# VectorE's block transposes in place of TensorE's for attention outputs and token rows

## The reference, cut to what matters

```python
xn = (x - mean) / sqrt(var + 1e-5)
# linear attention, 16 heads of 8, 64 features a head
q, k, v = heads(xn @ Wq + bq), heads(xn @ Wk + bk), heads(xn @ Wv + bv)
qp = relu(einsum('bhsd,hdf->bhsf', q, rw)) + 1e-6
kp = relu(einsum('bhsd,hdf->bhsf', k, rw)) + 1e-6
kv = einsum('bhsf,bhsd->bhfd', kp, v)
out = einsum('bhsf,bhfd->bhsd', qp, kv) / (einsum('bhsf,bhf->bhs', qp, kp.sum(2)) + 1e-6)
attn = out.reshape(b, s, 128) @ Wo + bo
# eight experts (128 -> 512 -> 128), each row goes to its best one
probs = softmax(xn @ wr + br); top_p, top_i = top_k(probs, 2)
gate = top_p[:, 0] / (top_p[:, 0] + top_p[:, 1])
ffn = gate * (gelu(xn @ w1[e] + b1[e]) @ w2[e] + b2[e])   # e = top_i[:, 0]
result = x + attn + ffn
```

## Time and profile before

| | us |
|---|---|
| median of 3 runs | 228.54 (228.49 to 228.83) |
| the profiled execution | 229.5 |
| its span, first to last instruction | 227.5 |

### The profile page before, as it was taken

One profiled execution on the slowest core, in us unless ns is written; L12 is line 12 of the kernel. 1 busy time (PEld: TensorE's weight loads), 2 busy tenths in 40 slices (PEclk: granted clock), 3 DMA queues, 4 the chain that ended last, 5 costly groups with the idle time before them and its releaser, 6 DMA issues. The chain is left out here.

```text
span 227.5 us, 6689 instructions
## 1 busy us (share of the span) xinstructions
PE 198.3 (87%) x2267; PEld 159.3 (70%) x2267; DVE 130.9 (58%) x420; ACT 124.0 (55%) x293; POOL 141.7 (62%) x165
## 2 busy tenths in 40 slices
PE   0399899589999999999999999999999999999930
PEld 0256466456666666666666666999999999999930
DVE  5737735959876667665665575345544455444420
ACT  3167797345654455544555565856666666666600
POOL 1847863022267777777777711018888888888885
PEclk9999999969999999999999999999999999999995
DMA  4945999950011111111112654168999999999331
GB/s 128 286 127 150 200 132 288 303 133 1 4 38 60 55 48 43 58 61 58 54 58 69 201 128 146 48 214 166 179 205 204 211 210 200 211 205 208 58 35 9
DMA packets 32191, 29.53 MB, mean 130 GB/s; under 512 B 5504, under 2 KB 24480, under 8 KB 32160
## 3 DMA queue, kind: packets, MB, share of 16 engines
q1 hardware_dynamic: 24752, 24.14, 40.6%
q0 software_dynamic: 6640, 4.24, 13.7%
q10 hardware_dynamic: 768, 0.74, 1.1%
HBM read 20.17 MB, written 11.49 MB: 139 GB/s over the span
## 5 line engine op out<-in xcount | busy, mean ns | idle before, releaser
L397 POOL DMA_INDIRECT out<-k_all,slots_all x39 | 61.0, 1563 | 25.4 <-DVE k_all L938 18.4
L715 ACT ACTIVATE q_all<-feat,w_slot 128x128 f32<-128x128 f32 x156 | 44.6, 369 | 28.4 <-PE feat L563 17.1
L372 POOL DMA_INDIRECT sorted_x<-rows_all,place_i x32 | 31.7, 990 | 15.6 <-PE kv_bank L471 8.4
L563 PE MATMUL feat<-v_all,w_slot 128*128 128x128 f32 x312 | 41.3, 275 | 0.0
L563 PEld LDWEIGHTS feat<-v_all,w_slot 128*128 128x128 f32 x312 | 38.0, 192 | 0.1
L672 ACT ACTIVATE k_feat<-feat 128x1024 f32<-128x1024 f32 x16 | 16.4, 1025 | 28.0 <-PE feat L449 28.0
L861 DVE TENSOR_SCALAR q_feat<-feat 128x1024 f32<-128x1024 f32 x16 | 19.6, 1225 | 16.2 <-PE feat L460 16.1
L679 ACT ACTIVATE q_feat<-feat 128x1024 f32<-128x1024 f32 x16 | 16.4, 1026 | 19.0 <-PE feat L460 19.0
L328 POOL TENSOR_SCALAR rows_all<-x_all,meanvar,rstd 128x128 f32<-128x128 f32 x23 | 18.7, 822 | 11.7 <-DVE rstd L747 11.7
L854 DVE TENSOR_SCALAR k_feat<-feat 128x1024 f32<-128x1024 f32 x16 | 19.6, 1224 | 10.6 <-PE feat L449 10.6
L460 PE MATMUL feat<-q_all,rw_bd 32*128 32x256 f32 x256 | 19.0, 411 | 7.4 <-DVE k_feat L854 7.4
(11 more groups left out here) (118 smaller groups left out, 313.0 us busy)
## 6 DMA issues: line engine op xcount, KB each, us to landing
w_slot<-w1x SPq DMA_DIRECT2D x39, 258.0 KB
sorted_x<-ones_f SPq DMA_DIRECT2D x1, 2535.0 KB, 17.6
x_all<-in_x SPq DMA_DIRECT2D x8, 256.0 KB, 3.8
w1x<-in_w SPq DMA_DIRECT2D x1, 2048.0 KB, 24.2
out<-res SPq DMA_DIRECT2D x16, 128.0 KB, 1.7
slots_all<-sorted_x SPq DMA_DIRECT2D x23, 65.0 KB
out<-k_all,slots_all POOLq DMA_INDIRECT x39
slots_all<-sorted_x SPq DMA_DIRECT2D x1, 520.0 KB, 5.8
```

Source lines behind the costliest of these rows:

```text
L372: pool.indirect_dma_start(sorted_x, bass.IndirectOffsetOnAxis(ap=place_i[:, t:t + 1], axis=0), rows_all[:, t, :], None).then_inc(x_moved, 16)
L397: pool.indirect_dma_start(out_rows, bass.IndirectOffsetOnAxis(ap=slot_rows[j % SLOT_RING][:, D + 1:XW].bitcast(I32), axis=0), y_sb[j % Y_R ...
L563: ins = pe.matmul(bank[:, a * P:(a + 1) * P], w1_slot[j % W1_RING][:, a * P:(a + 1) * P], xsT[j % X_RING][:, :], start=True, stop=True)
L715: act.activation(hidden_T[j % H_RING][:, a * P:(a + 1) * P], hid_bank[j % HID][:, a * P:(a + 1) * P], ACT.Gelu, bias=w1_slot[j % W1_RING][ ...
```

## The change

The outputs and token rows no longer go through TensorE's transposes and PSUM.

- save_outputs writes `pk` as blocks of 32 columns, the two parities side by side. token_rows is now four VectorE instructions on SBUF: a transpose of 128x512 in 32x32 blocks into `pk_tok`, the reciprocal of 32 columns, the multiply of 256, and a transpose of 128x256 into `attn_T`, which out_project reads directly. Three of them wait for the one before by a semaphore of VectorE's own.
- TensorE's turn_outputs is gone, and turn and save_turned carry the key-value matrix alone. out_project and residual come one iteration earlier (batch i-3).
- On VectorE, mask_kv(i-1) comes right after k_relu(i), in place of mask_kv(i) at the end of iteration i. count_slots, find_first, place_rows, place_gates, compare_slots and name_experts move from before q_relu to behind it, and token_rows too comes ahead of residual. The cast to `place_i` moves to the end of place_rows.
- GpSimd's loop is paced anew: in iteration i it waits for the key features, issues one scatter (i = 4 to 13; two at i = 14) and spread_v(i+1), waits for the query features, issues two scatters (i = 4 to 13) and out_bias(i-1). The output bias is added for four batches in each of the first four iterations.
- The sequence after the loop is rewritten on all engines, without turn(17) and turn(18).

```diff
@@ -23,6 +23,7 @@
 HD = D // NC
+TB = 2 * HD
 E, I = 8, 512
@@ -35,7 +36,9 @@
 PARTS = [(0, 2), (2, 8), (8, AHEAD)]
-MOVES = {b: 3 for b in range(3, 13)} | {13: 2}
+FIRST_MOVES = 4
+KF_MOVES = {i: 1 for i in range(FIRST_MOVES, 14)} | {14: 2}
+QF_MOVES = {i: 2 for i in range(FIRST_MOVES, 14)}
 SLOT_RING = AHEAD
@@ -109,10 +112,12 @@
         o_bias = [sb(f"o_bias{n}", [P, 2], F32) for n in range(2)]
-        ka = [sb(f"ka{n}", [P, 2 * S], F32) for n in range(2)]
-        pk = [sb(f"pk{n}", [P, 2, S], F32) for n in range(2)]
-        inv_den = sb("inv_den", [P, K * H], F32)
-        attn_tok = [sb(f"attn_tok{n}", [P, K, D], F32) for n in range(2)]
+        ka = [sb(f"ka{n}", [P, S], F32) for n in range(2)]
+        pk = [sb(f"pk{n}", [P, S // TB, 2, TB], F32) for n in range(2)]
+        pk_tok = sb("pk_tok", [P, 2 * S // TB, TB], F32)
+        inv_den = sb("inv_den", [P, 2 * S // TB, 2], F32)
+        attn_tok = sb("attn_tok", [P, S], F32)
+        attn_T = [sb(f"attn_T{n}", [P, S], F32) for n in range(2)]
@@ -197,10 +202,10 @@
         kf_ps, qf_ps, kv_ps, turn_ps = sem("kf_ps"), sem("qf_ps"), sem("kv_ps"), sem("turn_ps")
-        o_ps, pkT_ps, wo_ps = sem("o_ps"), sem("pkT_ps"), sem("wo_ps")
+        o_ps, wo_ps = sem("o_ps"), sem("wo_ps")
         k_act, k_dve, q_act, q_dve = sem("k_act"), sem("k_dve"), sem("q_act"), sem("q_dve")
         kv_ready, bias_ready, ka_ready, pk_ready = sem("kv_ready"), sem("bias_ready"), sem("ka_ready"), sem("pk_ready")
-        inv_ready, tok_ready = sem("inv_ready"), sem("tok_ready")
+        pk_turned, inv_ready, tok_scaled, tok_ready = sem("pk_turned"), sem("inv_ready"), sem("tok_scaled"), sem("tok_ready")
         r_ready, r_stored = sem("r_ready"), [sem(f"r_stored{u}") for u in range(R_RING)]
@@ -373,24 +378,33 @@
             pool.wait_ge(vro_in, 16 * 3)
-            for b in range(2):
-                spread_v(b)
+            spread_v(0)
             pool.wait_ge(xn_dve, CHUNKS)
...
             moved = [0]
-            for b in range(NBATCH):
-                out_bias(b)
-                if b + 2 < NBATCH:
-                    spread_v(b + 2)
-                add_out_bias(b)
-                if b == 3:
+
+            def moves(n):
+                for t in range(n):
+                    move(moved[0])
+                    moved[0] += 1
+
+            for i in range(NBATCH):
+                if i == FIRST_MOVES:
                     pool.wait_ge(placed, 2)
...
                     pool.wait_ge(mask_ready, 9)
-                for n in range(MOVES.get(b, 0)):
-                    pool.wait_ge((kf_ps, qf_ps, kv_ps)[n], b + 2)
-                    move(moved[0])
-                    moved[0] += 1
+                pool.wait_ge(kf_ps, i + 1)
+                moves(KF_MOVES.get(i, 0))
+                if i + 1 < NBATCH:
+                    spread_v(i + 1)
+                pool.wait_ge(qf_ps, i + 1)
+                moves(QF_MOVES.get(i, 0))
+                if i >= 1:
+                    out_bias(i - 1)
+                if i < FIRST_MOVES:
+                    for b in range(NBATCH // FIRST_MOVES * i, NBATCH // FIRST_MOVES * (i + 1)):
+                        add_out_bias(b)
+            out_bias(NBATCH - 1)
@@ -474,14 +488,9 @@
                 due(pe, ka_ready, i - 1)
-                if i <= NBATCH:
-                    pe.wait_ge(kv_ready, 2 * i)
-                    for par in range(2):
-                        ins = pe.transpose(kt_bank[:, par * P:(par + 1) * P], kv_T[(i - 1) % 2][:, par, :], ident[:, :])
-                if i >= 3:
-                    pe.wait_ge(tok_ready, i - 2)
-                    for k in range(K):
-                        ins = pe.transpose(kt_bank[:, S + k * P:S + (k + 1) * P], attn_tok[(i - 3) % 2][:, k, :], ident[:, :])
+                pe.wait_ge(kv_ready, 2 * i)
+                for par in range(2):
+                    ins = pe.transpose(kt_bank[:, par * P:(par + 1) * P], kv_T[(i - 1) % 2][:, par, :], ident[:, :])
                 ins.then_inc(turn_ps, 1)
@@ -489,7 +498,7 @@
                 pe.wait_ge(q_dve, b + 1)
-                due(pe, tok_ready, b)
+                due(pe, pk_ready, 2 * b)
                 for par in range(2):
@@ -497,19 +506,11 @@
-            def turn_outputs(b):
-                pe.wait_ge(pk_ready, 2 * (b + 1))
-                for k in range(K):
-                    for par in range(2):
-                        ins = pe.transpose(strided(o_bank[:, k * S + par * GD:k * S + par * GD + 1], [(2 * GD, G), (1, GD)]),
-                                           pk[b % 2][:, par, k * P:(k + 1) * P], ident[:, :])
-                ins.then_inc(pkT_ps, 1)
-
             def out_project(b):
-                pe.wait_ge(ka_ready, b + 3)
+                pe.wait_ge(tok_ready, b + 1)
                 due(pe, r_ready, b)
                 for k in range(K):
-                    ins = pe.matmul(wo_bank[:, k * D:(k + 1) * D], ka[(b + 3) % 2][:, S + k * P:S + (k + 1) * P], wo_sb[:, :],
+                    ins = pe.matmul(wo_bank[:, k * D:(k + 1) * D], attn_T[b % 2][:, k * P:(k + 1) * P], wo_sb[:, :],
                                     start=True, stop=True)
@@ -529,14 +530,12 @@
                     outputs(i - 2)
-                if i == 4:
-                    pe.wait_ge(placed, 2)
+                if i == 3:
+                    pe.wait_ge(placed, 1)
                     pe.wait_ge(wo_in, 16)
-                if i >= 4:
-                    out_project(i - 4)
+                if i >= 3:
+                    out_project(i - 3)
                 q_features(i)
-                if i >= 2:
-                    turn_outputs(i - 2)
                 if i >= 1:
@@ -580,26 +579,20 @@
             outputs(14)
-            pe.wait_ge(kv_ready, 2 * NBATCH)
+            turn(16)
             turn_slot(1)
-            turn(16)
-            out_project(12)
-            turn_outputs(14)
             out_project(13)
             outputs(15)
-            turn(17)
             up(0)
-            turn_outputs(15)
+            out_project(14)
             turn_slot(2)
             up(1)
-            out_project(14)
-            turn(18)
+            out_project(15)
             turn_slot(3)
...
             read_expert(0)
-            out_project(15)
             turn_slot(4)
-            pe.wait_ge(ka_ready, 18)
+            pe.wait_ge(pk_ready, 2 * NBATCH)
             down(0)
@@ -683,18 +676,15 @@
                 act.wait_ge(bias_ready, b + 1)
-                due(act, pkT_ps, b - 1)
+                due(act, pk_turned, b - 1)
                 for par in range(2):
-                    act.activation(pk[s][:, par, :], o_bank[:, par * S:(par + 1) * S], ACT.Identity,
+                    act.activation(pk[s][:, :, par, :], o_bank[:, par * S:(par + 1) * S].rearrange("p (t r) -> p t r", r=TB), ACT.Identity,
                                    bias=o_bias[s][:, par:par + 1]).then_inc(pk_ready, 1)
...
             def save_turned(i):
-                lo = 0 if i <= NBATCH else S
-                hi = 2 * S if i >= 3 else S
                 act.wait_ge(turn_ps, i)
                 due(act, o_ps, i - 2)
-                due(act, wo_ps, i - 4)
-                act.activation(ka[i % 2][:, lo:hi], kt_bank[:, lo:hi], ACT.Copy).then_inc(ka_ready, 1)
+                act.activation(ka[i % 2][:, :], kt_bank[:, 0:S], ACT.Copy).then_inc(ka_ready, 1)
@@ -719,10 +709,8 @@
             save_outputs(15)
-            save_turned(17)
             gelu(0)
             gelu(1)
-            save_turned(18)
             gelu(2)
@@ -831,9 +819,9 @@
                 then(dve.tensor_reduce(place_f[:, :], place_b[:, :, :].rearrange("p e t -> p t e"), AX.X, ALU.add))
+                dve.tensor_copy(place_i[:, :], place_f[:, :]).then_inc(placed, 1)
             def place_gates():
-                dve.tensor_copy(place_i[:, :], place_f[:, :]).then_inc(placed, 1)
                 dve.wait_ge(gate_exp, 1)
@@ -870,14 +858,18 @@
                 s = b % 2
-                dve.wait_ge(pkT_ps, b + 1)
-                dve.reciprocal(inv_den[:, :].rearrange("p (c h) -> p c h", h=2),
-                               strided(o_bank[:, HD:HD + 1], [(2 * HD, K * NC), (DK, 2)])).then_inc(inv_ready, 1)
+                dve.wait_ge(pk_ready, 2 * (b + 1))
+                dve.transpose(pk_tok[:, :, :].rearrange("p n r -> p (n r)"),
+                              pk[s][:, :, :, :].rearrange("p t a r -> p (t a r)")).then_inc(pk_turned, 1)
+                dve.wait_ge(pk_turned, b + 1)
+                dve.reciprocal(inv_den[:, :, :], strided(pk_tok[:, 0, HD:HD + 1], [(TB, 2 * S // TB), (DK, 2)])).then_inc(inv_ready, 1)
                 dve.wait_ge(inv_ready, b + 1)
-                due(dve, turn_ps, b + 1)
-                dve.tensor_tensor(strided(attn_tok[s][:, 0, 0:1], [(HD, K * NC), (DK, 2), (1, DK)]),
-                                  strided(o_bank[:, 0:1], [(2 * HD, K * NC), (DK, 2), (1, DK)]),
```

(33 more changed lines are left out.)

## The result

The changed kernel takes 231.63 us (median of 4 runs, 230.56 to 231.78) against 228.51 (228.49 to 228.83) for the kernel before on the same chip: a ratio of 1.0123 [1.0091, 1.0155]. The forecast was 229.4. The direction held, and so did the stated range of 226.2 to 232.5, but not the narrower 228.0 to 230.9 that the forecast gave itself: of the 3.1 us lost, it had 0.9.

A forecast was written before the change was run, and what follows sets the result against it. GpSimd's chain ends last, moved only by residual(14), behind the attention ring. Terms 2.87 + 0.70 + 0.39 - 2.63 + 0.13 - 0.60 = +0.86 took 228.54 to 229.4; range 226.2 to 232.5, the forecast's own 228.0 to 230.9.

The forecast's parts named there:

- One interval is 2.57 + 1.14 + X: Attention loop: VectorE's tail closes the ring; X, its token_rows and residual work before the next k_relu, 2.27; interval 5.98.
- batches 6 to 14: Eight steady loop intervals beside scatters: 47.84 against 50.47, so -2.63.
- The pieces before i = 2 stay: they wait for other things: Earliest loop iterations: no change in time, with count_slots behind q_relu(1) adding nothing.
- Two SBUF inputs: token_rows' multiply, reading both inputs from SBUF, collides with GpSimd's output-bias additions in i = 2 and 3: 0.7 for both.
- Batches 2 to 4: Loop intervals with place_rows and place_gates in VectorE's tail: 14.06 against 11.19, so +2.87.
- Batches 4 to 6: Loop intervals with compare_slots and name_experts in VectorE's tail: 13.03 against 12.64, so +0.39.
- Batch 14 to q_relu(15): End of the loop: 5.98 + 2.57 = 8.55 against 8.42, so +0.13.
- The way out: From q_relu(15) to the end of residual(14), after the loop: 9.95 against 10.54, so -0.60.
- Rival 1: VectorE's tail is shorter than sized, over 13 intervals and the loop's exit: 223.8, or 226.6 at half; chance 0.26.
- Rival 2: VectorE's own waits are held beside scatters, as TensorE's releases are: +4.5, so 233.9; chance 0.10.
- Rival 3: VectorE's transposes make two passes over the data: +0.8 x 14, so 240.6; chance 0.05.
- Rival 4: TensorE's clock falls in i = 2 or 3 after idling, about 1 more: 230.4 to 231.4; chance 0.09.

The follow-up runs named there:

- a_last: The changed kernel with the last two scatters split, one behind k_features(14) and one behind q_features(14): 230.70 us, ratio 1.0278.
- a_bias: The changed kernel with the output bias added for one batch per iteration, not four in each of the first four: 228.48 us, ratio 1.0221.
- after2: The changed kernel, unedited, profiled again on another chip: 231.54 us, ratio 1.0106 to the kernel before.
- before2: The kernel before, unedited, profiled again on another chip: 228.53 us, ratio 0.9989.
- a_all: The changed kernel with output bias for one batch per iteration, routing helpers before q_relu and the last two scatters split: 226.61 us, ratio 0.9901.
- after: The changed kernel, unedited, in its first measurement and profile: 231.63 us, ratio 1.0123 to the kernel before.
- a_split: a_all with 512 of VectorE's 1,024 columns of k_relu given to ScalarE: 225.90 us, ratio 0.9864.
- b_pace2: The same kernel as b_pace, measured again on a third chip: 231.73 us, ratio 1.0128.
- a_gap: The changed kernel with count_slots, find_first, place_rows, place_gates, compare_slots and name_experts back between mask_kv and q_relu: 226.81 us, ratio 1.0114.
- b_pace: The kernel before with only GpSimd's new loop, output bias one batch per iteration, last pair of scatters split: 224.51 us, ratio 1.0015.
- b_memset: The kernel before with each of the 32 scatters replaced by a GpSimd memset of about the same length: 223.63 us, ratio 0.9764.
- before: The kernel before, unedited, in the profile the prediction rests on: profiled execution 229.5 us, measured 228.51 beside the changed kernel.
- b_small: The kernel before with each scatter's rows cut from 130 numbers to 8, written to their own tensor: 228.91 us, ratio 1.0006.
- a_oldpace: The changed kernel with GpSimd's loop and pacing of the kernel before: 241.13 us, ratio 1.0523.

## Why the prediction was right in direction and short in size

- **The mechanism: right.** "One interval is 2.57 + 1.14 + X": X is 2.26 (2.27 forecast), the transposes 0.70 and 0.45 (0.71 and 0.44; 1.06 ns an element and 0.18 give 0.72 and 0.45), the interval 5.96 (5.98), batches 6 to 14 -2.76 (-2.63). One sign failed: ScalarE's k_relu was to be 0.5 or more ahead. It is 0.12 ahead on a chip with the hold, and 0.83 on the one without (a_last). The Trainium skill, "VectorE: DVE Perf Modes", "The three transpose paths", by which I estimated the same two figures, agrees with these fp32 rows.
- **"The pieces before i = 2 stay: they wait for other things": the step that failed**, for 1.46 of the 1.9 that the two profiles have over the forecast. count_slots behind q_relu(1) was priced at nothing, because "TensorE takes over 2 to the next key features". By itself that holds: in a_bias the helpers end at 51.85, ahead of VectorE's k_relu(2) at 52.06, 1.26 after the key features' start. With the four additions beside them it doesn't: 2.80 in after2, with no idle time ahead of k_relu(2). So the additions, beside helpers in this place, are the whole of this term: with them spread the interval is 5.21, below before2's 5.28.
- **"Two SBUF inputs": mis-located.** I looked only at the multiply, priced 0.35 twice, and it stretched from 0.43 to 0.54. In batch 1 the same kind of additions stretched four 8-column instructions by 0.27, 0.48, 0.49 and 0.47. I had read the Trainium skill, "SBUF — State Buffer", "Who interferes with whom", for two-input instructions alone. It also names cast and tensor_scalar, where their operands allow a two-port mode, and says that whichever engine issued first then blocks the other for its whole instruction. The four instructions above, each ending just after one of GpSimd's, agree with it; the multiply, stretched by 0.11 only, does not.
- **Batches 2 to 4: +3.12 against +3.57**, that is 0.45 less. The collision of the multiply, 0.22 in place of 0.70, is as much as that. place_rows in the tail cost 1.90 (59.52 to 61.42) against 1.89, but by luck: its second instruction took 0.74 beside spread_v in after2 and 0.43 in the changed kernel's first profile, its cast less than forecast.
- **Batches 4 to 6: +0.96 against +0.39.** In the tail of batch 5 the conversion of name_experts (39 columns, L836) took 0.78 beside a scatter, where I had 0.18. A scatter beside it isn't enough to explain that, as after2 and before2 show:

```profile
80.59 1.01 POOL L377 DMA_INDIRECT sorted_x<-rows_all,place_i  x1 [0.71 <-PE feat L463]
80.94 0.78 DVE L836 TENSOR_SCALAR expert_no<-expert_f 128x39 int32<-128x39 f32 x1
```

```profile
70.93 1.03 POOL L372 DMA_INDIRECT sorted_x<-rows_all,place_i  x1 [0.15 <-issue]
...
71.28 0.18 DVE L848 TENSOR_SCALAR expert_no<-expert_f 128x39 int32<-128x39 f32 x1
```

- **Batch 14 to q_relu(15): +0.66 against +0.13.** I wrote for batches 6 to 13 that no scatter is in flight when q_features ends, and took it for batch 14 too. Behind k_features(14) two are issued, and in after2 the second, at 130.84 to 131.80, is. The query features that started at 130.69 reached the relu at 132.45, 1.76 later. a_all, where the pair is split, has 2.56 from k_relu to q_relu there, after2 3.12.
- **The way out: -1.09 against -0.60**, mis-sized: 9.54 and not 9.95. token_rows(14) started at 4.95 and not 5.1 behind q_relu(15), and save_outputs(15) was over at 7.06 and not 7.6, so that token_rows(15) started right behind residual(13), at 7.21.
- **Rival 1, a shorter tail**: no, X is 2.26. **Rival 2, VectorE's own waits held**: no; the multiply starts 0.03 after the reciprocal (104.32, 104.35), 0.73 into the second scatter. **Rival 3, two passes**: no, 0.70. **Rival 4, TensorE's clock**: it did fall in the changed kernel's first profile, and cost next to nothing. The windows of the changed kernel (stretch, busy us of PE, PEld, DVE, ACT, POOL, granted clock, DMA share, GB/s):

```profile
52.00:55.00 3.00, 1.42 (x24) 0.43 (x19) 2.86 (x5) 1.85 (x3) 1.80 (x3) 1.00 0.16 5
55.00:58.00 3.00, 2.56 (x34) 1.69 (x38) 2.02 (x7) 1.19 (x2) 1.04 (x3) 0.71 0.00 0
58.00:61.00 3.00, 3.00 (x52) 2.01 (x48) 2.83 (x8) 0.48 (x2) 2.53 (x4) 0.72 0.02 5
```

After 1.42 us of work in 3, TensorE had parts of the next two stretches at 1.2 GHz, and k_relu(2) to q_relu(2) was 2.75 in place of 2.57. k_relu(3) then waited for VectorE, not for TensorE. In after2 the same step took 2.57.

The ring's mechanism is shown, but the direction was in part luck. With the multiply's collision and the way out sized as measured (0.22 and -1.09) the sum would have been about -0.1, no change at all. What made the kernel slower by more are the terms priced at nothing or too low. The upper end of the stated range, too, was room for rivals that didn't come true.

## What to carry to other kernels

When work moves to the engine that closes a ring, price that engine's whole tail in every iteration, the one-off pieces of the first ones too: here the loop gained 2.8 us in its eight steady iterations and lost 5.5 from batch 1 to batch 6. Small instructions of VectorE from SBUF to SBUF should not stand beside a row of GpSimd instructions, since each can wait for a whole one. Don't issue scatters from GpSimd back to back across a TensorE release that something waits for, and measure both kernels on the same chip.

## What the runs showed of the hardware that was not expected

- An indirect DMA issued by GpSimd delays TensorE in two ways, seen apart and together. The release of the 32-row matmuls of the key features comes late: 1.21 becomes 1.8 to 2.0, and 3.47 beside three back to back. And a row of matmuls is interrupted: the outputs take about 1.6 and not 1.07 in after, after2, a_all and a_split, the key features 1.7 and not 1.15 in b_pace2. A memset of like length does neither, and a sixteenth of the bytes leaves the late release as it is. By what path, stays open.
- It is there on two of the three chips of the experiments and absent on the third, in all four profiles of it (a_bias, a_gap, a_last, b_pace): there the kernel before takes 224.33 and not 228.8. Each chip was used on one occasion, so chip and occasion can't be told apart; what differs stays open.
- A VectorE conversion of 39 columns can wait for a whole instruction of GpSimd. Alone it takes 0.18. In a_all, a_split, b_pace and b_pace2 it took 0.38 to 0.55 and ended 0.04 or 0.05 after a GpSimd addition or spread_v; in b_memset it took 1.93 (71.33 to 73.26) and ended 0.04 after two memsets in a row. Beside a scatter it goes both ways: 0.77 and 0.78 in after and after2, ending about 0.1 after the scatter, and 0.18 inside one in before, before2, b_small and a_oldpace. What decides that stays open.
